# Layer 5's last sums of four blocks by TensorE with diagonal matrices; layer 6's weights sent one by one behind later tiles

## The chip, the cores and the metric

The kernel runs on one core of one Trainium2 chip. The metric is the device time of one execution in microseconds (us), as the median of several runs. TensorE (PE) multiplies matrices, with its weight loads shown apart as PEld. VectorE (DVE), ScalarE (ACT) and GpSimd (POOL) do the element-wise work, and SyncE (SP) issues most of the transfers (DMAs).

## What is computed

The reference is a decoder of twelve layers on a state of 8 blocks, each 128 tokens by 256 values. Each layer adds its result to the state and normalizes it. The change is in layer 5, a mixture of experts. Every token picks 4 of 32 large experts and, with each, the small expert that two large ones share. Its result is the sum over the four picks, each weighted by the token's share `w` of it:

```python
logits = x2d @ gate_w.T
rw = jax.nn.softmax(logits.astype(jnp.float32), axis=-1)
scores = jax.nn.sigmoid(logits.astype(jnp.float32))
_, sel = jax.lax.top_k(scores, TOP_K)            # TOP_K = 4
w = jnp.take_along_axis(rw, sel, axis=-1)
w = w / w.sum(axis=-1, keepdims=True)
...
g = jnp.einsum('th,ehi->eti', x2d, Wg)
u = jnp.einsum('th,ehi->eti', x2d, Wu)
a = jax.nn.silu(g) * u * cw.T[:, :, None]
return jnp.einsum('eti,eih->th', a, Wd)
...
x = _layernorm(x + _L1_ffn_ref(x, ...))          # layer 5
x = _layernorm(x + _L2_attn_ref(x, ...))         # layer 6
```

## The kernel before

Layer 5 (the class `DispatchedExperts`) sorts the tokens by expert. Each token's row is scattered to a buffer `xs` in DRAM, and 63 tiles of 128 rows are then worked off, each tile with one large and one small expert. In step s of the loop:

- SP has loaded the tile's rows `xg` (132.5 KB, a ring of three buffers) with `sp_load`. It may issue load i when tile i-3 has been turned (`xupright`) and its destinations are known (`directed`).
- PE turns the hidden values of tile s-1 (`pe_turn_a`), multiplies tile s with its gate and up weights (`pe_gate`), turns the rows of tile s+1 (`pe_turn_x`) and multiplies tile s-1 with its down weights (`pe_down`).
- ACT does the silu of tile s (`act_silu`), copies the turned rows of tile s+1 (`act_copy_x`) and copies the result of tile s-1 out (`act_copy_y`). In steps 0 to 7 it also issues one load of 512 KB each, the weights of the later experts, on its own queue. They are waited for at step 19 (`LATE`).
- DVE makes the products, copies and destination rows. In steps 4 to 10 it also makes the shares (`dve_shares`).
- POOL scatters the results to `zs` in DRAM (`pool_put`), so that the four results of one token stand side by side.

After tile 8 SP calls `layers[6].sp_weights`, which issues the six loads of layer 6's weights (256 KB each) in a row on the queue of the row loads. They go to the tile `CR`.

When all results are out, SP loads them back as `G[b]`, 512 KB for each of the 8 blocks, into `W`. DVE's `dve_combine` then makes the sum of a block: four instructions, each `G[:, j, :]` times the share, added to what there is (the first one to the state `X`), and then the mean and variance of the block (`bn_stats`, `bn_aggr`). POOL makes the reciprocal deviation (`pool_rstd`), DVE normalizes (`dve_norm`), PE turns the new state in the one bank kept for it (`pe_turn_state`), and ACT copies it to `XT` (`act_copy_state`). Blocks 0 to 3 are done this way at the end of layer 5. Blocks 4 to 7 are done within layer 6, between DVE's first steps there. Layer 6's first matmuls need blocks 0 to 3 of `XT` and its weights.

Every engine has one list of instructions, in the order in which the code writes them, and semaphores hold an engine until its inputs are there. `T.x.at(n)` means that the n-th step of kind x is done. An engine never skips over a waiting instruction.

Of the kernel before, what the change touches and what calls it, by code (L numbers as in the profile page):

```python
# [15 lines left out]
ACT = mybir.ActivationFunctionType  # L16
# [188 lines left out]
def build(nc, A, out):  # L205
    with ExitStack() as ctx:
        def sb(name, shape, dt=F32):
            return ctx.enter_context(nc.sbuf_tensor(name, shape, dt))
# [7 lines left out]
        XT = sb("XT", [128, 2, 1024])  # L216
# [22 lines left out]
        banks = [ctx.enter_context(nc.psum_tensor(f"ps{i}", [128, 512], F32))[:, :] for i in range(8)]  # L239
# [44 lines left out]
        s_rot = sem("s_rot")  # L284
        s_xg, s_put, s_z = s_sh, [sem(f"s_put{i}") for i in range(2)], s_b + [sem(f"s_z{i}") for i in range(5)]
# [9 lines left out]
        def cfc(n):  # L295
            return cf[:, CF[n][0]:CF[n][1]]
# [4 lines left out]
        ident = cfc("id")  # L301
# [38 lines left out]
        N = {}  # L340
# [61 lines left out]
        def pe_turn_state(e, l, b):  # L402
            e.wait_ge(*N[l].normed.at(b + 1))
            need_state_bank(e, l, b)
            tp(e, state_bank(l)[:, 0:128], X[:, b, 0:128])
            tp(e, state_bank(l)[:, 128:256], X[:, b, 128:256]).then_inc(N[l].xturned.sem, 1)
# [2047 lines left out]
        class DispatchedExperts:  # L2454
# [3 lines left out]
            def __init__(self, l):  # L2458
                self.l = l
                base = 2 * 2304 + 2 * RFN  # L2460
                self.rf = CR[:, 2 * 2304:base].bitcast(F32)
                self.rb = CR[:, base:base + RBN]
                room = Room((CR[:, base + RBN:2 * 3584].bitcast(F32), (2 * 3584 - base - RBN) // 2),
                            (AR0[:, 10240:11312], 1072))

                def blocks(n, dt=F32):
                    return room.take(8 * n, dt).rearrange("p (b e) -> p b e", b=8)

                self.share, self.rows = blocks(4), blocks(4).bitcast(I32)
                self.lg, self.mk, self.mS, self.ex = blocks(32), blocks(32, BF16), blocks(32), blocks(32)  # L2470
                self.macc = [room.take(32, BF16) for _ in range(2)]
                self.pad, self.cut, self.best = room.take(40), room.take(8), room.take(8)
                self.m, self.s = room.take(8), room.take(8)
                self.n, self.t, self.back, self.edge = room.take(32).bitcast(I32), room.take(32), room.take(32), room.take(33)
                self.below, self.hit, self.start = (room.take(w) for w in (33, 32, 32))
                self.prod, self.offsets, self.tab = room.take(96), room.take(3), room.take(3).bitcast(I32)
                self.wide, self.own = room.take(128), room.take(TILES)
                self.same, self.dest = room.ring(3, 4), [a.bitcast(I32) for a in room.ring(3, 1)]
                self.to = room.take(1)
                self.equal = XT[:, 0, :].rearrange("p (b j e) -> p b j e", b=8, j=4)  # L2480
                tiles = Room((AR0[:, 8192:10240], 2048))
                self.sg, self.a, self.aL, self.aS = tiles.ring(2, 224), tiles.ring(2, 224), tiles.ring(2, 128), tiles.ring(2, 128)
                rings = Room((Y[:, :, :].rearrange("p b n -> p (b n)"), 2048))
                self.xg, self.xt, self.yg = rings.ring(3, ROW), rings.ring(2, 256), rings.ring(2, 256)
                self.G = [W[:, 2 * (b // 4), 1024 * (b % 4):1024 * (b % 4 + 1)] for b in range(8)]
                n = TILES
                self.T = stage(logits=8, kept=8, chosen=8, counted=8, ranked=8, slots=8, totals=1, tabled=1, lessmax=1, lexped=1,
                               shares=1, widened=1, startsup=1, owned=1, xupright=n, xcopied=n, gate=n, silued=n, prod=n,
                               aturned=n, acopied=n, down=n, ycopied=n, directed=n, collected=8)
                self.router = smc("r1")  # L2490

            def rfc(self, n):
# [28 lines left out]
            def sp(self, e):  # L2521
                T = self.T
                for k, o in ((9, 0), (7, 4096), (8, 8192)):
                    e.wait_ge(*released[k])
                    e.e.dma_start(WL[:, o:o + 4096], A["gl"][:, o:o + 4096]).then_inc(s_large, 16)
                e.wait_ge(*N[3].added.at(8))
                e.e.dma_start(AR1[:, :], A["gs"]).then_inc(s_large, 16)
                e.wait_ge(*T.tabled.at(1))
                for i in range(TILES):
                    self.sp_load(e, i)  # L2530
                    if i == 8:
                        layers[6].sp_weights(e)
                for i in range(2):
                    e.wait_ge(s_put[i], 16 * ((TILES + 1 - i) // 2))
                for b in range(8):
                    e.e.dma_start(self.G[b], zs[128 * TILES + 512 * b:128 * TILES + 512 * (b + 1), :].rearrange("(p j) n -> p (j n)", j=4)).then_inc(s_z[b], 16)
# [77 lines left out]
            def pe(self, e):  # L2614
                T = self.T
                self.pe_rank(e, 7)
                self.pe_totals(e)
                e.wait_ge(s_large, 16 + 64)
                e.wait_ge(*T.tabled.at(1))
                self.pe_starts(e)  # L2620
                at = {0: self.pe_offsets(0)}
                self.pe_turn_x(e, 0)
                for s in range(TILES + 1):
                    if s == LATE:
                        e.wait_ge(s_late, 32 + 16 * 8)
                    if s >= 1:
                        self.pe_turn_a(e, s - 1)
                    if s < TILES:
                        self.pe_gate(e, s, at[s])
                    if s + 1 < TILES:  # L2630
                        at[s + 1] = self.pe_offsets(s + 1)
                        self.pe_turn_x(e, s + 1)
                    if s >= 1:
                        self.pe_down(e, s - 1, at.pop(s - 1))
                for b in range(4):
                    pe_turn_state(e, self.l, b)

            def dve_keep(self, e, b):
                T = self.T
# [156 lines left out]
            def dve(self, e):  # L2796
                self.dve_keep(e, 7)
                self.dve_choose(e, 7)
                self.dve_slots(e, 7)
                self.dve_table(e)  # L2800
                self.dve_less(e)
                self.dve_own(e)
                for s in range(TILES + 1):
                    if s < TILES:
                        self.dve_same(e, s)
                    if s >= 1:
                        self.dve_copy_a(e, s - 1)
                    if s < TILES:
                        self.dve_direct(e, s)
                        self.dve_prod(e, s)  # L2810
                        self.dve_dest(e, s)
                    if 4 <= s < 11:
                        self.dve_shares(e, s - 4)
                for b in range(4):
                    self.dve_combine(e, b)
                    if b:
                        dve_norm(e, self.l, b - 1)
                dve_norm(e, self.l, 3)
# [20 lines left out]
            def act(self, e):  # L2839
                T, l = self.T, self.l  # L2840
                e.wait_ge(*N[l - 1].added.at(8))
                e.wait_ge(*T.lessmax.at(1))
                e.act(self.ex, self.ex, ACT.Exp).then_inc(T.lexped.sem, 1)
                self.act_copy_x(e, 0)
                for s in range(TILES + 1):
                    if s < TILES:
                        self.act_silu(e, s)
                    if s + 1 < TILES:
                        self.act_copy_x(e, s + 1)
                    if s < 8:  # L2850
                        o = 12288 + 1024 * s
                        e.e.dma_start(WL[:, o:o + 1024], A["gl"][:, o:o + 1024]).then_inc(s_late, 16)
                    if s >= 1:
                        self.act_copy_y(e, s - 1)
                for b in range(4):
                    act_copy_state(e, l, b)

# [107 lines left out]
        class RotaryAttention:  # L2965
# [18 lines left out]
                self.T = stage(ones=1, made=24, taken=24, roped=8, keyed=16, scored=32, maxed=32, exped=32, turned=32,  # L2984
                               copied=32, valued=32, divided=8, upright=8, lifted=8, biased=8, wout=8)

            def sp_weights(self, e):
                e.wait_ge(*N[self.l - 2].added.at(8))
                for i, w in enumerate(self.wq):
                    e.e.dma_start(w, A["wrot"][:, 512 * i:512 * (i + 1)]).then_inc(s_rot, 16)  # L2990

            def made(self, n, x, c2, rot):

# [1443 lines left out]
```

## Time and profile before

| | us |
|---|---|
| median of 3 runs | 1880.52 (1879.43 to 1880.63) |
| the profiled execution's own time | 1876.53 |
| its span, first to last instruction | 1874.7 |
| PE busy | 1671.8 (89%) |
| DVE busy | 1199.1 (64%) |
| ACT busy | 938.6 (50%) |
| POOL busy | 662.2 (35%) |

All times of day below are microseconds from the start of this span. The tiles of layer 5 run from about 840 to 1034, its end with the first four sums from there to 1055, and layer 6 follows. Within the tiles PE is busy nearly all the time. The granted TensorE clock is shown as a share of 2.4 GHz: 1.00 is 2.4 GHz, 0.50 is 1.2 GHz. A transposition or a matmul in f32 leaves two records of PE for each instruction of the program.

### The profile page before, as it was taken

To read this page: it belongs to the slowest core of one execution; us is meant where nothing else is said; L and a number is where in the kernel's file an instruction comes from. 1 tells how busy PE (TensorE), PEld (TensorE's weight loads), DVE (VectorE), ACT (ScalarE), POOL (GpSimd) and SP (SyncE) were. 2 spreads that over 40 slices of the span, in tenths; PEclk is the share of its full clock that TensorE was granted. 3 is DMA by queue.
4 is the path that set the end of the run, shared out by engine and by line. 5 is a ranking of instruction groups with operands and counts; after the bars stand their busy time and mean duration, and the time that the engine had idled before them with its cause. 6 is when DMAs were issued, how large, how long until landed. Compare 5 with 4: busy or idle time off the path is not lost. (4 is left out here: it accounts for less than half of the span.)

```text
span 1874.7 us, 29412 instructions
## 1 busy us (share of the span) xinstructions
PE 1671.8 (89%) x10235; PEld 1264.6 (67%) x10249; DVE 1199.1 (64%) x2964; ACT 938.6 (50%) x2264; POOL 662.2 (35%) x819
## 2 busy tenths in 40 slices
PE   7998999899999989848999498869999879999996
PEld 6886677778888854427888156658888445555785
DVE  4555677567777765645555647874545668888766
ACT  3213788355555557722333036643333398888342
POOL 1104221223333241432333244432221348878412
PEclk9998999899999989979999799879999889999898
DMA  6003500283660042116333410003323010000020
GB/s 238 29 29 89 126 2 10 88 293 125 225 216 1 1 167 110 39 58 193 95 93 90 155 81 1 1 3 121 102 95 96 1 42 1 1 1 1 1 80 34
DMA packets 38263, 146.70 MB, mean 78 GB/s; under 512 B 6091, under 2 KB 21195, under 8 KB 33861
## 3 DMA queue, kind: packets, MB, share of 16 engines
q1 hardware_dynamic: 30244, 126.26, 19.8%
q0 software_dynamic: 6288, 14.18, 2.5%
q10 hardware_dynamic: 1584, 4.39, 0.8%
q8 instruction: 83, 1.36, 0.3%
q14 instruction: 64, 0.52, 0.1%
HBM read 126.33 MB, written 54.29 MB: 96 GB/s over the span
## 5 line engine op out<-in xcount | busy, mean ns | idle before, releaser
L182 PE MATMUL ps<-R 128*128 128x512 f32 (+2 forms) x3024 | 533.2, 341 | 23.6 <-DVE R L188 10.3
L182 PEld LDWEIGHTS ps<-R 128*128 128x128 f32 (+1 forms) x3024 | 441.5, 193 | 101.0 <-issue 17.0
L185 ACT ACTIVATE AR<-AR 128x128 f32<-128x128 f32 (+3 forms) x547 | 264.8, 557 | 122.4 <-DVE AR L199 93.9
L188 POOL TENSOR_TENSOR R<-W,R 128x768 fp32r<-128x768 f32 (+2 forms) x66 | 107.4, 1635 | 317.0 <-ACT R L2386 181.3
L308 PEld LDWEIGHTS ps<-cf,AR 128*128 128x128 f32 (+4 forms) x1023 | 124.8, 145 | 126.4 <-issue 52.4
L182 PE MATMUL ps<-AR 64*128 64x128 f32 (+5 forms) x1342 | 197.4, 317 | 8.6 <-DVE AR L188 7.6
L308 PE MATMUL ps<-cf,AR 128*128 128x128 f32 (+4 forms) x1023 | 176.5, 286 | 27.1 <-ACT AR L185 10.7
L182 PE MATMUL ps<-W,AR 128*128 128x256 f32 (+3 forms) x1152 | 192.4, 347 | 7.9 <-ACT AR L1600 7.9
L202 DVE TENSOR_TENSOR_SCAN AR<-AR,ps 128x512 f32<-128x512 f32 x128 | 154.0, 1215 | 33.7 <-PE ps L308 24.2
L188 POOL TENSOR_TENSOR AR<-AR,CR 128x512 f32<-128x512 f32 x128 | 161.5, 1275 | 36.2 <-DVE AR L202 35.6
L182 PEld LDWEIGHTS ps<-AR 128*128 128x128 f32 (+2 forms) x1342 | 147.1, 184 | 35.6 <-issue 23.7
L182 PEld LDWEIGHTS ps<-W,AR 128*128 128x128 f32 (+2 forms) x1152 | 145.9, 161 | 35.5 <-issue 16.9
L188 POOL TENSOR_TENSOR AR<-AR 128x512 f32<-128x512 f32 (+2 forms) x90 | 90.9, 1010 | 182.3 <-DVE AR L188 161.2
L188 DVE TENSOR_TENSOR AR<-ps,AR 128x512 f32<-128x512 f32 (+6 forms) x186 | 82.1, 468 | 95.4 <-PE ps L182 72.1
L182 PE MATMUL ps<-AR,cf 128*128 128x512 f32 x256 | 131.4, 596 | 0.1
L185 ACT ACTIVATE AR<-ps 128x224 f32<-128x224 f32 (+2 forms) x125 | 56.7, 458 | 127.7 <-PE ps L182 125.9
L2872 POOL DMA_INDIRECT zs<-Y,AR x63 | 60.4, 959 | 140.6 <-ACT Y L2837 135.9
L188 DVE TENSOR_TENSOR AR<-AR 128x2 f32<-128x2 f32 (+3 forms) x215 | 104.3, 486 | 3.7 <-ACT AR L185 0.8
L410 ACT COPY XT<-ps 128x256 f32<-128x256 f32 x80 | 29.9, 374 | 141.2 <-PE ps L308 135.9
L199 DVE TENSOR_REDUCE AR<-AR 128x4 f32<-128x512 f32 (+2 forms) x200 | 94.1, 474 | 7.4 <-DMA zs<-Y,AR 4.1
L2414 ACT CAST R<-AR 128x512 fp32r<-128x512 f32 x68 | 42.1, 621 | 113.2 <-DVE AR L188 113.2
L192 POOL TENSOR_SCALAR rs<-mv 128x1 f32<-128x1 f32 x96 | 24.6, 256 | 203.0 <-DVE mv L377 170.7
(261 smaller groups left out, 2767.9 us busy)
## 6 DMA issues: line engine op xcount, KB each, us to landing
xs<-in_zero SPq DMA_DIRECT2D x33, 1060.0 KB, 32.7
W<-in_wts SPq DMA_DIRECT2D x6, 1920.0 KB, 8.9
Y<-xs SPq DMA_DIRECT2D x63, 132.5 KB, 2.1
W<-in_wts SPq DMA_DIRECT2D x4, 2048.0 KB, 8.4
AR<-shd SPq DMA_DIRECT2D x16, 512.0 KB, 3.7
W<-in_wts SPq DMA_DIRECT2D x5, 1280.0 KB, 7.7
WL<-in_gl SPq DMA_DIRECT2D x3, 2048.0 KB, 12.2
AR<-in_gs SPq DMA_DIRECT2D x1, 6144.0 KB, 31.5
```

Of the source, the lines that this page charges most:

```text
L182: return self.e.matmul(o, l, r, start=start, stop=stop, skip_group_check=True)
L185: return self.e.activation(o, i, f, bias=bias, scale=scale)
L188: return self.e.tensor_tensor(o, a, b, op)
L192: return self.e.tensor_scalar(o, a, s1, None, op0)
L199: return self.e.tensor_reduce(o, i, AX, op, negate=negate)
L202: return self.e.tensor_tensor_scan(o, a, b, initial, op0, op1)
L308: return e.e.transpose(o, i, ident[0:n, 0:n])
L410: e.e.copy(XT[:, :, tok(b)], state_bank(l).rearrange("p (c n) -> p c n", c=2)).then_inc(N[l].xt.sem, 1)
L2414: e.e.copy(self.AH[i % 2], self.tb[i % self.HELD]).then_inc(T.rounded.sem, 1)
L2872: e.e.indirect_dma_start(zs[:, :], bass.IndirectOffsetOnAxis(ap=self.dest[i % 3], axis=0), self.yg[i % 2], None).then_inc(s_put[i % 2], 16)
```

## The change

The sums of blocks 0 to 3 move from DVE to PE. For each block b and pick j a matrix `D[b][j]`, 128 by 128, is made that has the shares of the 128 tokens on its diagonal. ACT makes the 16 of them, one in each of the steps 16 to 31, behind the copy of the result, out of the identity with the share as the scale. They lie in `XT`, which nothing uses until the new state comes. After the last tile PE multiplies: `pe_gather` makes four matmuls of 256 columns for a block, into bank 0 or 1, where they add up. DVE's `dve_combine` for these blocks becomes `dve_add`, one addition of the state to the bank, followed by the same mean and variance. Blocks 4 to 7 stay with `dve_combine`. PE's four `pe_turn_state` now stand behind all four `pe_gather`.

Apart from this, the six loads of layer 6's weights are issued one behind each of the loads of tiles 24 to 29, where they all stood behind the load of tile 8.

```diff
+                self.D = [[XT[:, j // 2, 256 * b + 128 * (j % 2):256 * b + 128 * (j % 2 + 1)] for j in range(4)] for b in range(4)]
...
                 for i in range(TILES):
                     self.sp_load(e, i)
-                    if i == 8:
-                        layers[6].sp_weights(e)
+                    if 24 <= i < 30:
+                        layers[6].sp_weights(e, i - 24)
...
                 for b in range(4):
+                    self.pe_gather(e, b)
+                for b in range(4):
                     pe_turn_state(e, self.l, b)
+
+            def pe_gather(self, e, b):
+                T, G = self.T, self.G[b].rearrange("p (j n) -> p j n", j=4)
+                e.wait_ge(*T.spread4.at(4 * b + 4))
+                e.wait_ge(s_z[b], (96 if b < 3 else 0) + 16)
+                e.wait_ge(*N[self.l].added.at(b - 1))
+                for j in range(4):
+                    t = e.mm(banks[b % 2][:, 0:256], self.D[b][j], G[:, j, :], j == 0, j == 3)
+                t.then_inc(T.gathered4.sem, 1)
...
                 for b in range(4):
-                    self.dve_combine(e, b)
+                    e.wait_ge(*self.T.gathered4.at(b + 1))
+                    dve_add(e, self.l, b, banks[b % 2][:, 0:256])
                     if b:
                         dve_norm(e, self.l, b - 1)
...
                     if s >= 1:
                         self.act_copy_y(e, s - 1)
+                    if 16 <= s < 32:
+                        b, j = divmod(s - 16, 4)
+                        e.wait_ge(*T.shares.at(1))
+                        e.act(self.D[b][j], ident, ACT.Identity, scale=self.share[:, b, j:j + 1]).then_inc(T.spread4.sem, 1)
...
-            def sp_weights(self, e):
+            def sp_weights(self, e, i):
                 e.wait_ge(*N[self.l - 2].added.at(8))
-                for i, w in enumerate(self.wq):
-                    e.e.dma_start(w, A["wrot"][:, 512 * i:512 * (i + 1)]).then_inc(s_rot, 16)
+                e.e.dma_start(self.wq[i], A["wrot"][:, 512 * i:512 * (i + 1)]).then_inc(s_rot, 16)
```

The next rows are SP's list in the kernel before, at the loads of tiles 7 to 10. `Y<-xs` is a row load, `CR<-in_wrot` a load of layer 6's weights.

```order
L2519 DMA Y<-xs 128x265
L2515 TENSOR_LOAD CR
L2519 ISA
L2519 DMA Y<-xs 128x265
L2990 DMA CR<-in_wrot 128x512 x6
L2515 TENSOR_LOAD CR
L2519 ISA
L2519 DMA Y<-xs 128x265
```

The same list in the changed kernel, at the loads of tiles 24 to 26.

```order
L2520 DMA Y<-xs 128x265
L3006 DMA CR<-in_wrot 128x512
L2516 TENSOR_LOAD CR
L2520 ISA
L2520 DMA Y<-xs 128x265
L3006 DMA CR<-in_wrot 128x512
L2516 TENSOR_LOAD CR
L2520 ISA
L2520 DMA Y<-xs 128x265
```

The block of six has gone from tile 8, and one such load now follows each of six row loads.

PE's list before, from the end of the last tile into layer 6. `ps<-cf,X` are the turns of the state, two for a block, and `ps<-XT,CR` are layer 6's first matmuls.

```order
L182 MATMUL ps<-WL,AR 128x256
L182 ISA
L182 MATMUL ps<-AR 128x256
L308 MATMUL ps<-cf,X 128x128 x8
L182 MATMUL ps<-XT,CR 128x512 x6
```

PE's list in the changed kernel at the same place.

```order
L182 MATMUL ps<-WL,AR 128x256
L182 ISA
L182 MATMUL ps<-AR 128x256
L182 MATMUL ps<-W,XT 128x256 x16
L308 MATMUL ps<-cf,X 128x128 x8
L182 MATMUL ps<-XT,CR 128x512 x6
```

Sixteen matmuls stand between the last tile and the turns.

DVE's list before, the sums of blocks 2 and 3. `Y<-W,CR` are the weighted sums, L193 the normalization of the block before.

```order
L196 SCALAR_TENSOR_TENSOR Y<-W,CR,X 128x256
L196 SCALAR_TENSOR_TENSOR Y<-W,CR,Y 128x256 x3
L2792 BN_STATS stt<-Y 128x6
L2794 BN_AGGR mv<-stt 128x2
L193 TENSOR_SCALAR X<-Y,mv,rs 128x256
L196 SCALAR_TENSOR_TENSOR Y<-W,CR,X 128x256
L196 SCALAR_TENSOR_TENSOR Y<-W,CR,Y 128x256 x3
```

And in the changed kernel, block 3 and what follows it.

```order
L188 TENSOR_TENSOR Y<-ps,X 128x256
L375 BN_STATS stt<-Y 128x6
L377 BN_AGGR mv<-stt 128x2
L193 TENSOR_SCALAR X<-Y,mv,rs 128x256 x2
L196 SCALAR_TENSOR_TENSOR AR<-ps,sm,cf 128x512
L196 SCALAR_TENSOR_TENSOR Y<-W,CR,X 128x256
```

Each block's four sums have become one addition that reads a bank; the sum of block 4 still stands behind layer 6's first step.

## Rows read from the trace of the kernel before

**Rows 1.** The page: busy time of PE and DVE over the span.

```profile
PE 1671.8 (89%) x10235; PEld 1264.6 (67%) x10249; DVE 1199.1 (64%) x2964; ACT 938.6 (50%) x2264; POOL 662.2 (35%) x819
```

**Rows 2.** Timeline, ACT, silus of tiles: start, duration, [idle before <-what ended it].

```profile
867.43 0.36 ACT L185 ACTIVATE AR<-ps 128x224 f32<-128x224 f32 x1 [0.89 <-PE ps L182]
878.46 0.36 ACT L185 ACTIVATE AR<-ps 128x224 f32<-128x224 f32 x1 [2.31 <-PE ps L182]
881.33 0.36 ACT L185 ACTIVATE AR<-ps 128x224 f32<-128x224 f32 x1 [1.41 <-PE ps L182]
```

**Rows 3.** Timeline, SP's issues around tile 8.

```profile
853.80 0.33 SPq L2519 DMA_DIRECT2D Y<-xs  x1
...
860.18 0.33 SPq L2519 DMA_DIRECT2D Y<-xs  x1
860.56 3.40 SPq L2990 DMA_DIRECT2D CR<-in_wrot  x6
864.52 0.34 SPq L2519 DMA_DIRECT2D Y<-xs  x1
```

**Rows 4.** Timeline, PE, turns of the rows of tiles 6, 8 and 9.

```profile
858.58 0.44 PE L308 MATMUL ps<-cf,Y 128*128 128x128 f32 x2 [0.74 <-DMA Y<-xs]
...
864.35 0.38 PE L308 MATMUL ps<-cf,Y 128*128 128x128 f32 x2
...
873.35 0.69 PE L308 MATMUL ps<-cf,Y 128*128 128x128 f32 x2 [5.96 <-DMA Y<-xs]
```

**Rows 5.** Stretches: busy PE, PEld, DVE, ACT, POOL, then PEclk, DMA share, GB/s.

```profile
852.00:856.00 4.00, 4.00 (x24) 3.24 (x23) 2.01 (x11) 1.61 (x5) 1.40 (x2) 1.00 0.88 284
868.00:872.00 4.00, 0.00 (x0) 0.00 (x0) 1.06 (x5) 0.00 (x0) 0.25 (x1) 0.84 1.02 387
877.00:878.00 1.00, 1.00 (x5) 0.94 (x4) 0.00 (x0) 0.00 (x0) 0.87 (x1) 0.73 0.00 0
900.00:920.00 20.00, 20.00 (x113) 16.76 (x112) 10.31 (x56) 6.78 (x22) 6.71 (x7) 1.00 0.32 96
1058.00:1059.00 1.00, 1.00 (x3) 0.51 (x2) 0.15 (x1) 0.00 (x0) 0.00 (x0) 0.77 0.00 0
1068.00:1070.00 2.00, 1.33 (x3) 0.82 (x4) 1.93 (x4) 0.37 (x1) 0.46 (x1) 0.67 0.00 0
```

**Rows 6.** Row loads from 880 to 1030, from issue to landing.

```profile
DMA to landing us min/median/max: 2.1/2.1/3.2
```

**Rows 7.** Groups by form, ACT, the nearest 128x128 scaled activation.

```profile
L185 ACT ACTIVATE AR<-AR,sm 128x128 f32<-128x128 f32 x16 | 5.4, 386 | 0.0
```

**Rows 8.** Timeline, all engines, from the last tile to layer 6's first step.

```profile
1033.28 0.60 PE L182 MATMUL ps<-AR 128*128 x2
...
1041.26 0.48 DVE L196 SCALAR_TENSOR_TENSOR Y<-W,CR,X 128x256 f32<-128x256 f32 x1 [8.66 <-issue]
...
1051.83 0.43 DVE L2792 BATCH_NORM_STATS2 stt<-Y 128x6 f32<-128x256 f32 x1
1052.29 0.18 DVE L2794 BATCH_NORM_AGGREGATE mv<-stt 128x2 f32<-128x6 f32 x1
...
1054.07 0.66 PE L308 MATMUL ps<-cf,X 128*128 128x128 f32 x2 [0.55 <-DVE X L193]
1054.77 0.37 ACT L410 COPY XT<-ps 128x256 f32<-128x256 f32 x1 [0.84 <-PE ps L308]
1055.25 0.29 PEld L182 LDWEIGHTS ps<-XT,CR 128*128 128x128 f32 x1 [0.93 <-issue]
...
1058.85 0.75 DVE L196 SCALAR_TENSOR_TENSOR AR<-ps,sm,cf 128x512 f32<-128x512 f32 x1 [4.90 <-PE ps L182]
```

**Rows 9.** Timeline, DVE, layer 6's additions behind two f32 matmuls of 256 columns each.

```profile
1086.38 0.42 DVE L188 TENSOR_TENSOR AR<-ps,sm 128x256 f32<-128x256 f32 x1 [0.44 <-PE ps L182]
1087.24 0.42 DVE L188 TENSOR_TENSOR AR<-ps,sm 128x256 f32<-128x256 f32 x1 [0.44 <-PE ps L182]
```

**Rows 10.** Timeline, PE, a turn in layer 6 at which the clock had fallen.

```profile
1068.67 0.69 PE L308 MATMUL ps<-cf,X 128*128 128x128 f32 x2 [2.82 <-DVE X L193]
```

More of the change, by code:

```diff
@@ L2488, in __init__ @@
                                shares=1, widened=1, startsup=1, owned=1, xupright=n, xcopied=n, gate=n, silued=n, prod=n,
-                               aturned=n, acopied=n, down=n, ycopied=n, directed=n, collected=8)
+                               aturned=n, acopied=n, down=n, ycopied=n, directed=n, spread4=16, gathered4=4)
                 self.router = smc("r1")
```

## The prediction

> **What bounds the kernel now.** I read the page first: PE is busy 89% of the span, DVE 64% [rows 1]. So PE's idle time and its slow clock are worth looking for, and I took the two places that the change touches.
>
> The first is the tiles. The silus of two tiles in a row are 2.87 us apart in the steady part (878.46 to 881.33), and a stretch of 20 us there has PE busy for all of it at the full clock [rows 2, 5]. So PE sets the tiles' pace. In one place two silus are 11.03 us apart (867.43 to 878.46) [rows 2]. The turn of tile 9's rows ended a wait of 5.96 us for its row load, at 873.35 [rows 4]. SP had issued six loads of 256 KB from 860.56, which took it 3.40 us, and tile 9's row load only then, at 864.52 [rows 3]. From 868 to 872 the DMA engines are full at 387 GB/s, PE does nothing, and the clock begins to fall. It is back at 2.4 GHz at about 877.5: the mean of 0.73 from 877 to 878 is 0.54 us at half clock [rows 5]. The place costs 11.03 - 2.87 = **8.16 us**, 5.96 of it the wait and the rest the slow clock after it.
>
> The second is the end of layer 5. The first sum starts at 1041.26, when the results are back, and the mean and variance of block 3 at 1051.83, 10.57 us later [rows 8]. That is four blocks of four sums of 0.48 us, with what stands between them. PE has no matmul to make in that time, only turns. Block 3's turn is at 1054.07, layer 6's first matmul loads at 1055.25, and DVE gets its result at 1058.85 [rows 8]. That takes 3.6 us because PE is at 1.2 GHz: the rise comes only from 1058 to 1059 [rows 5].
>
> **The change, part 1: the six weight loads.** At tile 8 they go. Tile 9's row load is then issued one period after tile 8's, at 860.18 + 2.87 = 863.05, and is needed one period after the turn of tile 8, at 864.35 + 2.87 = 867.2 [rows 3, 4]. It has 4.2 us. A row load takes 2.1 us when the DMA engines are at 96 GB/s [rows 5, 6]. Under ACT's loads of 512 KB, at 284 GB/s, tile 6's took 858.58 - 853.80 = 4.8 us and held PE by 0.74 us [rows 3 to 5]. It was the only such hold among tiles 3 to 8. Tiles 9 and 10 still meet ACT's last two loads. Best case: no hold, all 8.16 us return. Worst: only the 4.06 us that 1.57 MB take at 387 GB/s and SP's 1.47 us of late issue (864.52 - 863.05) go, so the load lands at 873.35 - 5.5 = 867.8 or, if both do not add up, 869.3. PE is held for up to 2.1 us, too short for the clock to fall: 6.1 us return. I take one hold in six for each of two tiles, 0.3 us: **gain 7.9 us**, bounds 6.1 and 8.2.
>
> The Trainium skill, "DMA: Bandwidth & Descriptors", section on queues, rings and completion order, says that each DMA engine takes turns between the queues it has work for, packet by packet. By it tile 9's load would share only with ACT's queue, and the sum would be 8.2 instead of 7.9; no row here tells the queues apart.
>
> At tiles 24 to 29 each weight load follows a row load on SP's queue. Issuing costs SP 3.40 / 6 = 0.57 us of a period of 2.87, in which it does one other load. The 262 KB take 0.68 us at 387 GB/s, and the next row load is issued 2.87 us later. Even if all of it delayed a row load, 2.1 + 0.7 = 2.8 us is under the 4.2 us that a load has. ACT's loads are twice as large at the same rhythm and gave one hold of 0.74. I take 0; the bound is one hold, 0.7. Layer 6 needs the weights at 1055, over 100 us later.
>
> **Part 2: the diagonal matrices.** ACT makes 16 at 0.39 us each [rows 7]. Before each silu ACT is idle for 1.41 us, waiting for PE [rows 2], and the new instruction stands in that gap behind the copy. Cost 0. If it failed to fit, it would be 16 x 0.39 = 6 us. It overruns only if it takes over 1.4 us. The list of ACT in the changed kernel has no further table load.
>
> **Part 3: the sums.** DVE loses four sums of 0.48 a block [rows 8] and gets one addition of 0.42. PE gets four f32 matmuls of 256 columns a block. In layer 6 two such matmuls let DVE start every 0.86 us (1086.38 to 1087.24) [rows 9], so four are 1.72 us at the full clock and 3.44 at half. PE has been idle since 1033.9 [rows 8], longer than before tile 9, so it starts at half. Two restarts show how long that lasts: 873.35 to 877.5 is 4.1 us, and 1055.3 to about 1058.5 is 3.2 us [rows 4, 5, 8]. I take 3.7. Sixteen matmuls are 6.88 us of full-clock work, 3.7 us of it at half speed add 1.85: 8.7 us. The 0.16 us until DVE sees the result (3.60 less twice 1.72, as worked out below) and the 0.42 of its addition come on top, so block 3's statistics start 9.3 us after the first result is back, against 10.57: **gain 1.2 us**, 1.0 and 1.5 by the two restarts. DVE's share of a block (0.42 + 0.43 + 0.18 and a normalization of about 0.4, 1.4 us) [rows 8, 9] fits beside PE's 1.72. The waits of the third and fourth sum for their bank ask for the addition two blocks back, which is earlier by 1 us. Results of blocks 1 to 3 arrive every 1.4 us (512 KB at 387 GB/s is 1.35 us [rows 5]), sooner than PE asks.
>
> The turns of blocks 0 to 3 are queued on PE behind all of this. At the full clock a turn and its copy take about 0.95 us (0.44 and 0.37, and 0.15 between them, from 1055.25 less 1054.77 and the like) [rows 4, 8], so turn 3 could start 2.85 us after the last sum. Its normalized block is ready 0.59 + 2.24 (1051.83 to 1054.07) = 2.83 us after it [rows 8]. The queue costs nothing, and no margin is left. At half clock the cycle is 1.2 us, and turn 3 is 0.75 us late.
>
> **Then the clock.** The sums leave PE warm. The turns have gaps of 0.6 us between them; the rows show the clock fallen by 1070 after an idle time of 2.82 us [rows 5, 10], and not after short gaps within the tiles. If it holds, turn 3 takes 0.44 instead of 0.69 us (**0.25**), and the first result of layer 6 takes 1.9 us instead of 3.6, since its two matmuls of 512 columns are twice the work of the 0.86 us above, 1.72 us at the full clock (**1.7**). DVE is then busy with blocks 4 to 7, so that this shift carries on. Part 3 is 1.2 + 0.25 + 1.7 = **3.1 us**.
>
> [...]
>
> **Sum:** 7.9 + 3.1 = 11.0 us. The profiled execution would go from 1876.5 to 1865.5. The runs' median is 4.0 us above that execution, so I subtract the gain from the median: 1880.5 - 11.0 = **1869.5**. What makes the 4.0 us the trace cannot show. Its bounds: part 1 from 5.4 (6.1 less one hold) to 8.2, part 3 from 0.4 to 3.4. Later places where DVE waits for a half-clock PE can shift by 1.7 either way.
>
> **Rivals.**
> 1. *The clock falls between the sums and layer 6.* Between the last sum and layer 6 PE has only four short turns in 3.6 us, and in the place where the clock had fallen by 1070 it had also worked on and off before. Then the 1.95 us go and turn 3 is 0.75 late: part 3 gives 0.4, in all 8.3, **1872.2**. Chance 0.22.
> 2. *PE stays at half clock through the sums.* 13.8 us instead of 8.7 and slow turns: part 3 costs 4.6, in all 3.3 us gained, **1877.2**. Against it: both restarts rose. Chance 0.06.
> 3. *The long hold is mostly of the profiled execution.* The other runs have it smaller, and only part 3 stays: **1877.4**. Against it: they are slower, not faster. Chance 0.05.
> 4. *Slower: the weight loads hold tiles 24 to 29 as they held tile 9.* Each is on the queue ahead of the next row load. Holding tile 9 took six of them plus late issue. It decides from 11.0 / 6 = 1.8 us a tile, when a row load takes 5.8 us and not 2.1. At 3.0 us a tile it costs 18.0 against the 11.0 gained: **1887.5**. Chance 0.04.
> 5. *The change doesn't do what it says* (tile 9 held by ACT's loads alone): part 1 gives 0 to 2, **1876.5**. Against it: none of tiles 3 to 8 was held over 0.74. Chance 0.03.
>
> **Numbers.** A measurement tells some 0.2%, 3.8 us, from no change: 1876.8 to 1884.3. The forecast has 0.60, its own range 1866 to 1874. Faster: 0.60 + 0.22 + 0.03 = 0.85. Same: rivals 2 and 3, 0.11. Slower: rival 4. The range of 1865.5 to 1876.8 leaves out rivals 2 to 4 and a little of the forecast's ends.
>
> **What would show it.** Right: no wait for a row load over 1 us near tile 9 or from tile 24 to 30, silus 2.87 us apart there, the sixteen matmuls within about 8.7 us, layer 6's first records 0.43 us apart. Wrong: a wait for a row load behind ACT's loads, a silu that waits for ACT itself, a clock of 0.50 at layer 6's first matmul, or block 3's turn waiting for PE and not for DVE.

## The result

| | median, us | runs |
|---|---|---|
| before | 1879.93 (1870.67 to 1884.43) | 20 |
| changed | 1870.19 (1860.15 to 1879.72) | 20 |

The ratio of the changed kernel's time to that of the kernel before is 0.9959, with a 95% interval of 0.9944 to 0.9973. That is 7.7 us faster, between 5.1 and 10.5; the medians are 9.7 us apart. Forecast were 1869.5 and a gain of 11.0. The single runs of one kernel lie up to 20 us apart, so a difference of the size of the forecast's smaller terms has to be read from traces, place by place.

The profiled execution of the changed kernel took 1870.81 us, with a span of 1869.0. Where it differs from the trace of before:

| stretch | before, us | changed, us | difference |
|---|---|---|---|
| layers 0 to 4, to the first tile's silu (code unchanged) | 843.51 | 836.31 | -7.2 |
| first to last tile's silu | 187.25 | 179.61 | -7.6 |
| last silu to the first result back | 10.50 | 10.46 | 0.0 |
| first result back to layer 6's first step on DVE | 17.59 | 14.38 | -3.2 |
| from there to ACT's copy of the turned block 7 in layer 7 (code unchanged) | 184.26 | 198.97 | +14.7 |
| the rest (code unchanged) | 631.6 | 629.3 | -2.3 |

The two places that the change touches gave what was forecast for them. Between them and the end stand unchanged layers that differ by up to 15 us from one trace to the other.

### The profile page after: what moved, and what is told of

Read it like the earlier page. It is cut to its first block and busy times, and to the rows that moved or that the text cites. A ratio compares the mean times of both kernels' runs of the same rounds, so it can differ in the third digit from the quotient of the medians.

```text
span 1869.0 us, 29498 instructions
## 1 busy us (share of the span) xinstructions
PE 1684.3 (90%) x10281; PEld 1274.2 (68%) x10281; DVE 1195.9 (64%) x2952; ACT 943.9 (51%) x2280; POOL 661.8 (35%) x819
## 5 line engine op out<-in xcount | busy, mean ns | idle before, releaser
L182 PEld LDWEIGHTS ps<-R 128*128 128x128 f32 (+1 forms) x3024 | 442.8, 192 | 99.7 <-issue 15.1
L182 PE MATMUL ps<-AR 64*128 64x128 f32 (+5 forms) x1342 | 207.5, 329 | 7.2 <-DVE AR L188 7.1
L182 PE MATMUL ps<-W,AR 128*128 128x256 f32 (+3 forms) x1152 | 187.5, 338 | 7.9 <-ACT AR L1600 7.9
L182 PEld LDWEIGHTS ps<-AR 128*128 128x128 f32 (+2 forms) x1342 | 151.8, 190 | 36.3 <-issue 25.1
```

The source lines that it names most:

```text
L182: return self.e.matmul(o, l, r, start=start, stop=stop, skip_group_check=True)
```

## The profile after

**The tiles.** The timeline of ACT in the changed kernel, silus of tiles 8 and 9, then the diagonal matrix made in step 16 and the silu of tile 17; the columns are those of [rows 2].

```profile
860.75 0.36 ACT L185 ACTIVATE AR<-ps 128x224 f32<-128x224 f32 x1 [1.42 <-PE ps L182]
863.62 0.36 ACT L185 ACTIVATE AR<-ps 128x224 f32<-128x224 f32 x1 [1.41 <-PE ps L182]
...
885.08 0.40 ACT L185 ACTIVATE XT<-cf,CR 128x128 f32<-128x128 f32 x1
886.60 0.36 ACT L185 ACTIVATE AR<-ps 128x224 f32<-128x224 f32 x1 [1.11 <-PE ps L182]
```

Tiles 8 and 9 are 2.87 us apart, where [rows 2] has 11.03. Over all the tiles 7.6 of these 8.16 us are left, since tile 1 came 0.6 us late here. It does so in five of the nine traces with the sums on PE and in none of the five others; why is open. `XT<-cf,CR` is a diagonal matrix. It takes 0.40 us, and ACT still waits 1.11 us for PE before its silu: it lies wholly in the gap. The row loads at tiles 24 to 29 are as quick as in [rows 6]:

```profile
DMA to landing us min/median/max: 2.0/2.1/3.1
```

**The sums.** The timeline of the changed kernel, which answers to [rows 8], PE and DVE only.

```profile
1026.38 8.73 PE L182 MATMUL ps<-W,XT 128*128 128x256 f32 x32 [7.35 <-DMA W<-zs]
...
1035.14 0.42 DVE L188 TENSOR_TENSOR Y<-ps,X 128x256 f32<-128x256 f32 x1 [0.32 <-PE ps L182]
...
1035.60 0.43 DVE L375 BATCH_NORM_STATS2 stt<-Y 128x6 f32<-128x256 f32 x1
...
1037.80 0.42 PE L308 MATMUL ps<-cf,X 128*128 128x128 f32 x2 [0.55 <-DVE X L193]
...
1038.77 5.39 PE L182 MATMUL ps<-XT,CR 128*128 128x512 f32 x12 [0.55 <-ACT XT L410]
...
1040.76 0.75 DVE L196 SCALAR_TENSOR_TENSOR AR<-ps,sm,cf 128x512 f32<-128x512 f32 x1 [3.04 <-PE ps L182]
```

The sixteen matmuls (32 records) run without a gap for 8.73 us. Block 3's statistics start 9.2 us after the first result is back (10.57 before), and layer 6's first result comes 2.0 us after its first matmul (3.6 before). Now the stretches, as in [rows 5]:

```profile
1028.00:1029.00 1.00, 1.00 (x3) 0.80 (x3) 0.00 (x0) 0.00 (x0) 0.00 (x0) 0.50 1.05 430
1029.00:1030.00 1.00, 1.00 (x5) 0.79 (x4) 0.04 (x1) 0.00 (x0) 0.00 (x0) 0.70 1.01 401
1030.00:1031.00 1.00, 1.00 (x6) 0.90 (x5) 0.93 (x3) 0.00 (x0) 0.00 (x0) 1.00 1.02 414
1035.00:1038.50 3.50, 1.56 (x9) 0.69 (x7) 1.75 (x5) 1.36 (x4) 1.40 (x3) 1.00 1.01 431
```

PE starts at 1.2 GHz and is at 2.4 GHz from 1029.6, 3.2 us after its start. The clock then holds through the turns (last row), so that layer 6 begins at the full clock.

**Layers 6 and 7.** The same view over one long stretch, from layer 6's first step on DVE to the turn of block 7 in layer 7, first before, then changed.

```profile
1058.85:1243.11 184.26, 149.16 (x705) 101.71 (x713) 133.65 (x287) 87.16 (x263) 86.68 (x107) 0.88 0.06 25
```

```profile
1040.76:1239.73 198.97, 164.63 (x715) 112.07 (x713) 135.76 (x287) 88.42 (x263) 86.53 (x107) 0.81 0.06 23
```

The work is the same, DVE, ACT and POOL are busy for nearly the same time (DVE for 2.1 us more), and PE is busy for 15.5 us more at a mean clock of 0.81 instead of 0.88. At two levels, 1.00 and 0.50, the means say that the clock was low for some 44 us before and some 75 us here.

## The experiments

Two questions stood open: is each part's gain the one worked out, and does the change itself make layers 6 and 7 slower? The rival theory takes the 199 us of the trace for an effect of the change. Mine takes them for the clock, whose falls differ between any two executions.

**The weight loads alone.** The sums stay on DVE.

```diff
-                    if i == 8:
-                        layers[6].sp_weights(e)
+                    if 24 <= i < 30:
+                        layers[6].sp_weights(e, i - 24)
...
```

> Only the six weight loads are moved to tiles 24 to 29; the sums stay on DVE. The theory: the hold at tile 9 is the work of the six loads alone, so the silus of tiles 8 and 9 are 2.87 us apart (11.03 before), and from the first result's return to layer 6's first step on DVE it takes 17.6 us as before (1041.26 to 1058.85). Median 8 us below the kernel before, less or more what layers 6 and 7 add. The rival, that the change as such slows layers 6 and 7: from layer 6's first step on DVE to the first turned block of layer 7's second half it takes some 199 us, as in the changed kernel's trace, and not 184 as in the trace of before, and the median is within 3 us of the kernel before.

Measured: median 1870.57 us, ratio to the kernel before 0.9952 (0.9927 to 0.9976). Its timeline, ACT:

```profile
863.96 0.36 ACT L185 ACTIVATE AR<-ps 128x224 f32<-128x224 f32 x1 [1.41 <-PE ps L182]
866.84 0.36 ACT L185 ACTIVATE AR<-ps 128x224 f32<-128x224 f32 x1 [1.41 <-PE ps L182]
```

The hold is gone and 17.8 us pass from the first result's return to layer 6. Layers 6 and 7 took 189.4 us. This part alone gives the time of the whole change. It ran a second time, as the base of later kernels:

> The kernel in which only the weight loads are moved, once more, as the base for the next two on one chip. Both theories: about 1870 us, the silus of tiles 8 and 9 2.87 us apart, 17.7 us from the first result's return to layer 6's first step on DVE.

1869.81 us, ratio 0.9962 (0.9945 to 0.9979), 17.8 us, and 185.1 us for layers 6 and 7. The two ratios are 9.0 and 7.1 us for the weight loads, and their intervals together run from 4 to 14.

**The sums alone.** The changed kernel with the six loads back behind tile 8.

> Only the sums of blocks 0 to 3 are moved to PE; the six weight loads stay behind tile 8. The theory: tile 9 is held as before (silus 11 us apart), and from the first result's return to layer 6's first step on DVE it takes 14.4 us (17.6 before). Median 3 us below the kernel before, with layers 6 and 7 anywhere from 184 to 199 us. The rival, that moving the sums is what slows layers 6 and 7: 199 us there and a median 10 us above the kernel before.

Measured: 1876.99 us, ratio 0.9992 (0.9967 to 1.0018). The traces agree with the theory in place: 14.5 us from return to layer 6, and the hold is back. Its timeline, ACT, tiles 7 to 9:

```profile
863.28 0.36 ACT L185 ACTIVATE AR<-ps 128x224 f32<-128x224 f32 x1 [1.42 <-PE ps L182]
866.50 0.36 ACT L185 ACTIVATE AR<-ps 128x224 f32<-128x224 f32 x1
876.24 0.36 ACT L185 ACTIVATE AR<-ps 128x224 f32<-128x224 f32 x1 [1.72 <-PE ps L182]
```

9.74 us and not 11.03 between the last two: the hold is 6.9 us in this execution, and a further 0.35 at the tile before. The 10 us of loss that the rival asked for did not come, and neither did the 3 us of gain in the median. The interval, from 6 us faster to 3 us slower, still holds that gain.

**The same kernel again.**

> The changed kernel once more, to see what differs between two traces of one program. The theory: the silus of tiles 8 and 9 are 2.87 us apart and the sums take 14.4 us again, each within 0.5 us, while layers 6 and 7 come out anywhere from 184 to 199 us, by how long TensorE's granted clock is 0.50 there. The rival, that the change slows layers 6 and 7: 199 us again, within 2.

Measured: 1868.62 us, ratio 0.9954 (0.9927 to 0.9981). Tiles 2.87, sums 14.8, layers 6 and 7 191.3 us. The stretch:

```profile
1043.57:1234.91 191.34, 156.52 (x715) 105.88 (x713) 136.29 (x287) 87.77 (x262) 86.54 (x107) 0.85 0.06 24
```

So one program gives 199 and 191 us, with clocks of 0.81 and 0.85. The rival's fixed 199 falls.

**Six loads, where and how.** First one by one, but behind tiles 8 to 13, beside ACT's last loads; then all six in a row, but behind tile 24.

```diff
-                    if 24 <= i < 30:
-                        layers[6].sp_weights(e, i - 24)
+                    if 8 <= i < 14:
+                        layers[6].sp_weights(e, i - 8)
```

> The changed kernel, but with the six weight loads behind tiles 8 to 13, one behind each, so that the first ones still meet ACT's last loads. The theory, that the hold at tile 9 came from all six standing ahead of one row load: no hold over 1 us at tiles 9 to 14 (silus no more than 3.9 us apart). The rival, that any weight load beside ACT's loads holds the tiles: one or more gaps of 5 us or more between silus there.

> The changed kernel, but with all six weight loads in a row behind tile 24, long after ACT's loads. The theory: 1.57 MB at 387 GB/s are 4.1 us and SP issues the next row load 1.5 us late, so the row load of tile 25 takes 2.1 + 4.1 us and lands some 3.5 us after it is needed: silus of tiles 24 and 25 about 6.4 us apart. The rival, that only the six together with ACT's loads hold a tile: 2.87 us, or at most 3.9.

One by one, the widest distance between silus of tiles 8 to 14 is 3.00 us, between tiles 9 and 10, the second and the third row here:

```profile
866.00 0.36 ACT L185 ACTIVATE AR<-ps 128x224 f32<-128x224 f32 x1 [1.41 <-PE ps L182]
868.88 0.36 ACT L185 ACTIVATE AR<-ps 128x224 f32<-128x224 f32 x1 [1.21 <-issue]
871.88 0.36 ACT L185 ACTIVATE AR<-ps 128x224 f32<-128x224 f32 x1 [1.36 <-PE ps L182]
```

Six in a row behind tile 24, timeline of ACT at tiles 24 and 25, and PE's turn of tile 25's rows:

```profile
913.32 0.36 ACT L185 ACTIVATE AR<-ps 128x224 f32<-128x224 f32 x1 [1.12 <-PE ps L182]
918.45 0.36 ACT L185 ACTIVATE AR<-ps 128x224 f32<-128x224 f32 x1 [1.06 <-PE ps L182]
```

```profile
915.34 0.44 PE L308 MATMUL ps<-cf,Y 128*128 128x128 f32 x2 [2.06 <-DMA Y<-xs]
```

The distance is 5.13 us, a hold of 2.3 where 3.5 were expected. So the block of six holds a tile by itself. Beside ACT's loads the hold is three times as long, and long enough for the clock to fall; one at a time they hold nothing even there. It was the six standing together, not the bytes. Whether the row load waited for its turn in SP's queue or for a share of the full DMA engines, these runs do not tell apart: loads that are spread out change both. (As single runs, 1868.31 and 1882.98 us; the second has the longest layers 6 and 7 of all, 201.3 us.)

**A filled layer 6.** Matmuls whose results are overwritten are added in layer 6, to the changed kernel and to the one with the weight loads alone.

```diff
                                 if 2 <= m < 6:
+                                    for _ in range(6):
+                                        e.mm(banks[2], identb, cbc("mc"), True, True)
                                     pe_turn_state(e, 5, m + 2)
...
                         e.mm(k, identb, cbc("mc"), True, False)
+                        e.mm(k, identb, cbc("mc"), True, False)
```

> The changed kernel with matmuls in layer 6 whose results are overwritten: six of 512 columns (bf16) before each of the turns of blocks 4 to 7, and the matmul that adds the mask to the scores made twice, 32 more. They cost some 0.22 us each where PE is the one waited for, 7 us in all. The theory, that layers 6 and 7 differ from run to run by the time at 1.2 GHz: the clock is 1.00 more of the time there, and from layer 6's first step on DVE to layer 7's last but two blocks it takes 190 us or less, in spite of the added work. The rival, that the change slows layers 6 and 7 by something other than the clock: the added 7 us come on top, 198 us or more.

> The same matmuls added to the kernel in which only the weight loads are moved and the sums stay on DVE. The theory, that the sums' gain of 3 us stands once the clock varies less: its median is 3 us above that of the filled changed kernel. The rival, that moving the sums gives its 3 us back in layers 6 and 7: the two medians are within 1 us.

Measured: 1874.43 us (0.9980, 0.9962 to 0.9997) and 1874.99 us (0.9982, 0.9963 to 1.0002). Both traces have 193.7 us in layers 6 and 7. The clock was low for 53 us there, hardly less than elsewhere, and the fill cost 4 to 5 us. As a remedy this failed. The two medians are 0.6 us apart, as the rival said, but the first trace shows why it says little. In it the clock rose late, and fell again before layer 6:

```profile
1031.82 10.16 PE L182 MATMUL ps<-W,XT 128*128 128x256 f32 x32 [7.04 <-DMA W<-zs]
```

```profile
1043.00:1044.00 1.00, 0.45 (x4) 0.20 (x2) 0.42 (x2) 0.37 (x1) 0.71 (x2) 1.00 0.94 399
1044.00:1045.00 1.00, 0.45 (x4) 0.25 (x2) 0.41 (x1) 0.37 (x1) 0.15 (x1) 0.87 0.69 292
1045.00:1046.00 1.00, 0.45 (x3) 0.18 (x2) 0.00 (x0) 0.37 (x1) 0.00 (x0) 0.50 0.15 61
```

The matmuls took 10.16 us, since the rise came only 6.1 us after their start, and the fall at the last turn gave the slow first step of layer 6 back: 17.8 us in all, as with the sums on DVE. This is the first rival of the forecast.

It came in two more of the nine traces with the sums on PE. In the kernel with six loads behind tile 24 the clock fell at 1047.9, 0.9 us after layer 6's first matmul. In the second trace of the kernel kept warm, described next, it fell at 1042.2, at the end of block 3's turn. The stretches, in this order:

```profile
1048.00:1049.00 1.00, 1.00 (x3) 0.48 (x2) 0.00 (x0) 0.00 (x0) 0.00 (x0) 0.50 0.19 77
```

```profile
1042.00:1043.00 1.00, 0.45 (x3) 0.24 (x3) 0.00 (x0) 0.37 (x1) 0.00 (x0) 0.61 1.01 430
```

Layer 6's first result then took 2.9 and 3.8 us after its first matmul, and 3.8 in the filled kernel. In the six traces in which the clock held it took 2.0.

**PE kept warm.** In the changed kernel, 15 matmuls between the last tile and the first sum.

```diff
+                e.wait_ge(*T.spread4.at(16))
+                for i in range(15):
+                    e.mm(banks[0][:, 0:256], self.D[0][i % 4], XT[:, 0, 256:512], True, True)
                 for b in range(4):
                     self.pe_gather(e, b)
```

> The changed kernel with 15 more matmuls of 256 columns on PE between the last tile and the first sum, into the bank that the first sum overwrites; they fill the 7.4 us in which PE waits for the results (15 x 0.43 = 6.5 us at the full clock). The theory: PE is still at 2.4 GHz when the first result is back, the sixteen matmuls take 6.9 us instead of 8.7, and layer 6's first step on DVE is 12.6 us after the first result's return instead of 14.4. The rival, that the extra matmuls end late or that the sums wait for the results of blocks 2 and 3: 14 us or more there.

Measured: 1865.12 us, ratio 0.9919 (0.9886 to 0.9952). Its timeline, PE:

```profile
1023.01 6.64 PE L182 MATMUL ps<-XT 128*128 128x256 f32 x30
1030.06 3.72 PE L182 MATMUL ps<-W,XT 128*128 128x256 f32 x16 [0.41 <-DMA W<-zs]
1033.93 3.72 PE L182 MATMUL ps<-W,XT 128*128 128x256 f32 x16
```

PE waits 0.4 us instead of 7.4, and the sums run at the full clock. They take 7.6 us and not 6.9, since PE now waits 0.4 us between the second and the third block (3.87 us from start to start, where eight matmuls are 3.44). From return to layer 6 it is 13.3 us (12.6 expected). A second time:

> The changed kernel with 15 matmuls between the last tile and the first sum, once more. In the traces so far it takes 13.3 us where the sums on DVE take 17.7. The theory, that this gain stands at the end of the program: its median is 4.4 us below that of the kernel that moves the weight loads only, within 2. The rival, that layers 6 and 7 give the sums' gain back: within 2 us of it.

1868.50 us, ratio 0.9936 (0.9913 to 0.9959), with 14.8 us in its trace: the sums ran in 7.3 us, but the clock fell before layer 6's first result. Its median is 1.3 us below the base's, so this run speaks for the rival. Over both pairs of runs the mean is 3.5 us below that of the kernel with the weight loads alone, give or take 2.7 (20 and 24 executions).

**PE warm with the sums on DVE.** The weight loads moved, and 71 matmuls between the last tile and the turns.

> Only the weight loads are moved and the sums stay on DVE, but PE makes 71 matmuls of 512 columns (bf16), whose results are overwritten, in the time in which it waits for the results and between the turns, so that layer 6 begins at the full clock without the sums on PE. From the first result's return to layer 6's first step on DVE it should take 15.8 us, 1.9 less than with a cold PE. The theory, that a head start of about 2 us at layer 6 is lost again in layers 6 and 7 however it is gained: the median is within 1.5 us of the kernel without the extra matmuls (1870). The rival, that it is the sums on PE that cost something later: its median is 2 to 3 us below it, near 1867.5.

Measured: 1866.35 us, ratio 0.9937 (0.9913 to 0.9960), and 15.7 us in place. Its median is 4 us below the base's, its mean 2.4 us, give or take 3.4. That is on the rival's side, and not enough to decide. But its stretch of layers 6 and 7, with the sums on DVE, is one of the long ones. (The profiled execution, 1878.63 us, was the slowest of the eleven.)

```profile
1050.06:1246.71 196.65, 161.32 (x715) 109.89 (x713) 137.15 (x287) 88.21 (x263) 86.67 (x107) 0.83 0.06 23
```

**The tail of layers 6 and 7.** In the first kernel kept warm, seven groups of five matmuls before PE's waits at the end of these layers.

> The same kernel, and in the tail of layers 6 and 7, where PE waits for DVE and POOL and the clock is 0.50 for some 27 us in every trace, seven groups of five matmuls of 512 columns (bf16) before PE's waits, into a bank that is free there. The theory: the clock is 1.00 for most of the tail, layer 8 begins at the full clock, and the time is 2 to 4 us shorter than without them. The rival, that DVE and POOL set the tail's time and the groups delay PE's turns: no difference, or up to 4 us longer.

Measured: 1865.38 us, ratio 0.9944 (0.9922 to 0.9966), from 6 executions, of which the profiled one was the fastest (1859.96). The stretch of the tail in the kernel with the weight loads alone, and here:

```profile
1205.00:1233.00 28.00, 15.05 (x57) 11.23 (x57) 26.16 (x57) 11.22 (x31) 15.95 (x25) 0.52 0.00 0
```

```profile
1194.00:1221.00 27.00, 17.46 (x78) 10.18 (x80) 23.86 (x54) 9.82 (x28) 14.83 (x22) 0.82 0.00 0
```

The clock in the tail went from 0.52 to 0.82, and layers 6 and 7 took 186.5 us. The median is 3.1 us below that of the kernel kept warm from the same chip (1868.50), the ratio no better than its 0.9936, and the intervals overlap. Whether the tail gains is open.

**All traces without added work in layers 6 and 7.**

| kernel | sums on | layers 6 and 7, us | of it at 1.2 GHz, us |
|---|---|---|---|
| before | DVE | 184.3 | 44 |
| weight loads alone, again | DVE | 185.1 | 42 |
| six loads behind 8 to 13 | PE | 187.7 | 48 |
| weight loads alone | DVE | 189.4 | 50 |
| changed, again | PE | 191.3 | 58 |
| sums alone | PE | 192.1 | 58 |
| warm, again | PE | 192.1 | 64 |
| warm | PE | 192.6 | 61 |
| warm, sums on DVE | DVE | 196.7 | 68 |
| changed | PE | 199.0 | 75 |
| six loads behind 24 | PE | 201.3 | 76 |

The last column is worked out from the granted clock in stretches of 2 us. The time grows with it, by (201.3 - 185.1) / (76 - 42) = 0.48 us for each us at half clock; a straight line through all eleven gives 0.45. That is near the 0.5 of a stretch in which PE alone sets the pace. Kernels with the same placing of the sums stand far apart.

The placing of the sums does not fix the time. The two filled kernels have their sums on different engines, yet both began layer 6 after 17.8 us, and both took 193.7 us with 53 us at 1.2 GHz. In the table the three traces in which layer 6 began late, 17.6 to 17.8 us after the first result, took 184 to 189 us. The eight in which it began after 13.3 to 15.7 us took 188 to 201, the one with the sums on DVE included. So an early start goes with a low clock later, but this order is seen and not shown to be a cause.

**All executions.** Each execution has a mean granted clock, and with two levels the time at 1.2 GHz is 2 x (1 - clock) x span. In the 31 executions of the kernel before that ran beside the first experiments it goes with the total time (correlation 0.96), at 0.38 us for each us. So most of the spread between single executions goes with the clock. The 32 executions of the changed kernel have 211.1 us at 1.2 GHz, and the 24 with the weight loads alone 211.4, a difference of -0.3, give or take 5.3. Yet between the last silu and layer 6's first step the traces of the same kernels have only 7 and 10 us of it with the sums on PE, and 22 and 23 with them on DVE. From that step to the end they have 123 and 106 against 98 and 90. So some 14 us of low clock are saved at the end of layer 5 and come back behind it.

## Why the prediction was right, and where not

1. *Part 1, the hold of tile 9: 7.9 us.* Right. The trace shows the 8.16 us at tile 9 gone, and the weight loads alone measured 7.1 and 9.0 us. The cause was also the one named: the six in a row hold a tile in both places tried (2.3 us behind tile 24), and one by one they hold none, even where the first of them meet ACT's last loads. The remaining 0.3 us for tiles 9 and 10 was not needed. The bound on what a block costs without ACT's loads would have been too high (3.5 against 2.3).
2. *Part 1, tiles 24 to 29: 0.* Right. Row loads took 2.1 us in the median and 3.1 at most, and no distance between silus from tile 8 on was over 2.94 us. The slower rival, 1.8 us a tile, had nothing.
3. *Part 2, the diagonal matrices: 0.* Right: 0.40 us each (0.39 taken), with 1.11 us of waiting left.
4. *Part 3, in place: 3.1 us.* Right in this trace, 3.2, term by term: 8.73 us for the matmuls (8.7), 9.2 to the statistics (9.3), 2.0 for layer 6's first result (1.9), and turn 3 waits for the normalized block and not for the queue. As a typical value it was too high. Over the six traces with a cold PE and the sums on PE the time from return to layer 6 was 14.4, 14.5, 14.8, 15.1, 15.6 and 17.8, 15.4 in the mean; over the three with the sums on DVE and a cold PE besides before's, 17.8. The gain is 2.4. Two terms were mis-sized. One is the time to the rise: I took 3.7 us between 3.2 and 4.1, and the traces have 2.9 to 6.1, so that the matmuls took 9.2 us in the mean and not 8.7. Two restarts are too few to bound it. The other is the 1.7 us for a clock that holds until layer 6's first result. It held in four of these six traces, and in six of all nine with the sums on PE. In the other two the first result came 0.9 and 1.8 us later. The rival in which the clock falls there had a chance of 0.22.
5. *"This shift carries on."* This step is the one that did not hold. Over 32 executions with the sums on PE and 24 without, all with the weight loads moved, the mean differs by 0.8 us, give or take 2.1, to the wrong side; the sums alone against before differ by 0.0, give or take 3.3. A gain of 3.1 at the end of the program is excluded by the first comparison, one of 1.3 is not. The clock is what differs: the 14 us at 1.2 GHz that the sums on PE save at the end of layer 5 come back, in the mean of the 32 executions. At 0.38 us each that is worth some 5 us, an estimate, where the totals ask for 3.2 (2.4 and 0.8), give or take 2.1. Layers 6 and 7 are where the traces differ most. That they come out long more often with the sums on PE (seven traces from 188 to 201) than without (184, 185 and 189, but also 197) is seen. That the sums cause it is not shown. The long one without them speaks against it, and so do the two filled kernels with the same 193.7 us. Why the clock falls more often behind an early start of layer 6 stays open.
6. *The start from the median.* The 4.0 us between the first profiled execution and the median need no cause of their own: single executions of before spread from 1870.7 to 1884.4, and layers 0 to 4, unchanged, end anywhere from 836.3 to 845.4 us in the fourteen traces.
7. *The range and a price.* The bounds of the parts give gains of 5.8 to 11.6, so 1868.9 to 1874.7, and with 1.7 either way 1867.2 to 1876.4. The forecast's own range of 1866 to 1874 lies about 1 to 2 us too low. In the fourth rival a hold of 1.8 us a tile needs a row load of 4.2 + 1.8 = 6.0 us, not 5.8.

So the forecast's 11.0 became 7.7 to 9.7: part 1 came in full, and part 3 is local only. That 1869.5 came within 1 us of the measured 1870.19 is partly luck: the term that did not arrive was small, and single executions, of which three gave its starting point, lie up to 14 us apart.

## What to carry to other kernels

Large prefetches go one at a time between the small loads that a loop lives on, not in a row ahead of one of them: the same bytes cost 8 us as a block and nothing when spread. A wait of the engine that sets the pace can cost twice, once for itself and once for a restart at the low clock. Here 5.96 us of waiting cost 8.16, and a wait of 2.06 us left the clock as it was. Look in the trace for both. And where single executions spread by 20 us, judge a 3 us gain by its interval in several traces, then ask whether it is still there at the end. Here 3 us were not.

## What the runs showed of the hardware

- The granted clock is a source of spread by itself: with one program, unchanged layers took 191 or 199 us, and over eleven traces some 0.45 us longer for each us at 1.2 GHz. Over 31 whole executions of one kernel the slope is 0.38. The time from a restart of PE to the rise was between 2.9 and 6.1 us in the traces of the sums.
- The clock can fall when PE has just had only short turns with gaps of 0.55 us between them. It did so in three of nine traces: twice at the fourth turn, and once 0.9 us into the matmuls that follow. In the other six, with the same turns, it held.
- Doubling a bf16 matmul in each step of a loop that sets the pace did not keep the clock up (53 us at 1.2 GHz). Fifteen matmuls in a wait of 7.4 us kept it up through the sums in all three traces, and saved 0.6 to 2.6 us of the 15.4.
